# A graph layer on one NeuronCore: two folds of 1024 words become one of 2048, without a second place to fold into

## What is computed

```python
def layer(cur, incidence_m):
    mask = incidence_m > 0
    head = mask.astype(incidence_m.dtype)
    head = head / jnp.maximum(jnp.sqrt(jnp.sum(head * head, axis=-1, keepdims=True)), EPS)
    inc = incidence_m + head
    edge_fea = inc @ cur
    edge_degree = jnp.sum(inc, axis=-1, keepdims=True)
    return edge_fea / edge_degree

h = jnp.maximum(_layernorm(x, axis=-1), 0.0)
x = x + layer(h, adj)
```

## Time and profile before

| | |
|---|---|
| median of 3 runs | 1268.14 us (1267.59 to 1268.84) |
| profiled execution | 1278.49 us, its span 1276.7 us |
| DVE busy | 1189.2 us, 93% |
| ACT busy | 975.5 us, 76% |
| PE busy | 959.0 us, 75% |
| POOL busy | 791.1 us, 62% |
| DMA, moved | 471.00 MB, mean 369 GB/s |

### The profile page before, as it was taken

How to read it: one execution, slowest core, us unless ns; L and a number is a source line. 1 busy time by engine, 2 the same in 40 slices (tenths; PEclk the granted TensorE clock), 3 DMA queues, 4 the chain that set the end, 5 groups by cost and what they waited for, 6 DMA issues and landing times.

```text
span 1276.7 us, 14660 instructions
## 1 busy us (share of the span) xinstructions
PE 959.0 (75%) x2680; PEld 478.1 (37%) x2682; DVE 1189.2 (93%) x2868; ACT 975.5 (76%) x1902; POOL 791.1 (62%) x748
## 2 busy tenths in 40 slices
PE   0003878888888878787988887978878888977677
PEld 0001434444444444443434443434444434433343
DVE  6679999998999999998999999999999999999961
ACT  6657787887887988786888877888877888884731
POOL 1003667676666777776766767777776776765562
PEclk9999899898988989899898989999989988987888
DMA  9999999999999999999999999999999999997532
GB/s 356 427 422 406 396 394 388 369 387 369 379 378 382 401 373 401 395 401 394 402 400 401 392 374 384 399 400 395 402 396 402 402 397 373 401 390 275 175 106 74
DMA packets 148207, 471.00 MB, mean 369 GB/s; under 512 B 24826, under 2 KB 24826, under 8 KB 143965
## 3 DMA queue, kind: packets, MB, share of 16 engines
q1 hardware_dynamic: 90368, 331.38, 66.3%
q0 software_dynamic: 57744, 138.64, 29.7%
HBM read 490.47 MB, written 33.82 MB: 411 GB/s over the span
## 4 chain that ended last, share of the span: by engine, by line
DVE 55%; issue 17%; DMA 11%; ACT 6%; PE 6%; another core or an unknown queue 2%; SPq 1%; POOL 0%; DVEq 0%; ACTq 0%; POOLq 0%
DVE cand_word L794 17%; DVE folded L772 16%; DMA adj_tile<-in_adj_dram 8%; DVE cand_index L798 6%; DMA gathered_rows<-in_x_dram 3%; PE acc L1326 3%; DVE cand_index L817 2%; DVE cand_word L812 2%; ACT junk L573 2%; ACT adj_tile L560 2%; ACT diag L636 1%; PE acc L1337 1%; DVE diagonal_alone L779 1%; DVE entry L961 1%
## 5 line engine op out<-in xcount | busy, mean ns | idle before, releaser
L494 POOL DMA_INDIRECT gathered_rows<-h_scratch,slot_column x520 | 559.9, 1077 | 263.1 <-issue 158.0
L573 ACT ACTIVATE junk<-adj_tile,zero_unit 128x2048 bf16<-128x2048 f32 x256 | 510.0, 1998 | 48.3 <-issue 27.5
L1326 PE MATMUL acc<-gathered_rows,diag 128*128 128x512 f32 x1040 | 489.6, 622 | 21.4 <-DMA gathered_rows<-h_scratch,slot_column 18.2
L494 POOL DMA_INDIRECT gathered_rows<-h_scratch,spill_column x198 | 223.1, 1127 | 195.0 <-ACT spill_column L619 135.2
L794 DVE MAX8 cand_word<-folded 128x8 f32<-128x1024 f32 x244 | 298.2, 1222 | 5.9 <-remote 1.3
L772 DVE SCALAR_TENSOR_TENSOR folded<-adj_tile 128x1024 f32<-128x1024 f32 x244 | 296.1, 1214 | 7.7 <-DMA adj_tile<-in_adj_dram 5.6
L1326 PEld LDWEIGHTS acc<-gathered_rows,diag 128*128 128x128 f32 x1040 | 203.8, 204 | 263.4 <-issue 262.6
L798 DVE FIND_INDEX8 cand_index<-cand_word,folded 128x8 uint32<-128x1024 f32 x244 | 297.3, 1219 | 0.0
L1337 PE MATMUL acc<-gathered_rows,spill_matrix 128*128 128x512 f32 x396 | 186.8, 609 | 46.0 <-DMA gathered_rows<-h_scratch,spill_column 42.4
L636 ACT ACTIVATE diag<-ident,weights_and_payload 128x128 f32<-128x128 f32 x581 | 176.2, 388 | 16.0 <-issue 6.5
L1337 PEld LDWEIGHTS acc<-gathered_rows,spill_matrix 128*128 128x128 f32 x396 | 72.8, 192 | 154.8 <-issue 154.6
(11 more groups left out here) (151 smaller groups left out, 880.1 us busy)
## 6 DMA issues: line engine op xcount, KB each, us to landing
adj_tile<-in_adj_dram SPq DMA_DIRECT2D x256, 1024.0 KB
h_scratch<-adj_tile SPq DMA_DIRECT2D x16, 1024.0 KB, 10.6
out_dram<-out_tile SPq DMA_DIRECT2D x64, 256.0 KB
gathered_rows<-in_x_dram SPq DMA_DIRECT2D x12, 1024.0 KB, 12.6
x_residual<-in_x_dram SPq DMA_DIRECT2D x48, 256.0 KB
gathered_rows<-h_scratch,slot_column POOLq DMA_INDIRECT x520
x_held<-in_x_dram SPq DMA_DIRECT2D x4, 1024.0 KB, 7.9
gathered_rows<-h_scratch,spill_column POOLq DMA_INDIRECT x198, 3.5
```

The lines of the kernel that those rows point to most:

```text
L494: nc.gpsimd.indirect_dma_start(out=into, out_offset=None, in_=h[:, :], in_offset=bass.IndirectOffsetOnAxis(ap=column, axis=0), bounds_chec ...
L573: nc.scalar.activation(junk[:, n % 2].rearrange("p (j c) -> p j c", j=2), both[:, :, half], ACT.Relu, bias=zero_unit[:], scale=-UP, accum_ ...
L1326: last = nc.tensor.matmul(acc[t % 3][:], diag[:, t % 2, 1 + s], slot(t % 2, s), start=False, stop=False)
```

## The change

In each of the 61 folded tiles two folds take the place of four. `fold(t, k)` waits for chunks 2k and 2k + 1 and folds both in one operation of 2048 words, which fills both places of `folded`. So it also waits for the search of the chunk just before it, where a fold waited for the search of the chunk two before. The second fold of a period stands where the third stood; the fourth, between `heads` and `incs`, and the second, between `take_entry` and `columns_any`, are gone. The searches stay at 1024 words. In the diff's line numbers, those of the kernel after are two higher from the middle of `fold` on.

```diff
@@ load_chunk
-                        sp.wait_ge(folded, CHUNKS * (t - 2) + j + 1)
+                        sp.wait_ge(folded, 2 * (t - 2) + j // 2 + 1)
@@ fold
-            def fold(t, j):
-                dve.wait_ge(adj_loaded[t % 2][j], 16 * turn(t))
-                if CHUNKS * t + j >= 2:
-                    dve.wait_ge(idx_found, CHUNKS * t + j - 1)
-                a = chunk(t % 2, j)
-                nc.vector.scalar_tensor_tensor(out=F[:, j % 2], in0=a[:, 1], scalar=UP, in1=a[:, 0],
+            def fold(t, k):
+
+                for j in (2 * k, 2 * k + 1):
+                    dve.wait_ge(adj_loaded[t % 2][j], 16 * turn(t))
+                if 2 * t + k >= 1:
+                    dve.wait_ge(idx_found, CHUNKS * t + 2 * k)
+                a = A[:, t % 2, 4 * CW * k:4 * CW * (k + 1)].rearrange("p (j h c) -> p j h c", j=2, h=2)
+                nc.vector.scalar_tensor_tensor(out=F[:], in0=a[:, :, 1], scalar=UP, in1=a[:, :, 0],
                                                op0=ALU.mult, op1=ALU.add).then_inc(folded, 1)
-                if j == diag_chunk(t):
+                if k == diag_chunk(t) // 2:
                     read_diagonal(t)
                     cut_diagonal(t)
@@ cut_diagonal
-                dve.wait_ge(folded, CHUNKS * t + diag_chunk(t) + 1)
+                dve.wait_ge(folded, 2 * t + diag_chunk(t) // 2 + 1)
@@ find_values
-                dve.wait_ge(folded, CHUNKS * t + j + 1)
+                dve.wait_ge(folded, 2 * t + j // 2 + 1)
@@ period
                 if pick:
                     take_entry(r)
-                fold(t, 1)
                 if small:
                     columns_any(p)
                     ranks(p)
@@ period
                     pay_columns(p)
-                fold(t, 2)
+                fold(t, 1)
                 find_values(t, 2)
                 find_places(t, 2)
                 if small:
                     heads(p)
-                fold(t, 3)
                 if small:
                     incs(p)
                 find_values(t, 3)
```

## The result

The changed kernel takes 1272.64 us (median of 7 runs, 1270.72 to 1273.31), the kernel before 1268.58 in runs taken beside them (7 runs, 1267.28 to 1271.67). The ratio is 1.0028, with an interval of 1.0017 to 1.0039: 4.1 us slower. The profiled execution took 1273.31 us, its span is 1271.6.

What follows compares the result with a forecast made beforehand. DVE was taken to set the pace, busy 234 of 240 us. Fresh wait and folds 5.4, less 2.0 for diagonal tiles, plus 2.5 at the start gave 5.9: 1268.14 to 1274.0 us, 80% range 1267.5 to 1279.

Steps and rivals of the forecast that it cites:

- The large fold, heads and incs: Both pairs of a tile: 0.06 gained on the first, 0.07 lost on the second by incs waiting uncovered; 0.01 lost.
- The fresh wait: First fold of a pair waits for the search just before: 0.08 lost per tile; with both pairs 0.09, 5.4 us.
- The diagonal in chunk 3: In 13 tiles, fold to MAX8 and heads to MAX8 shorten by 0.16 more than in ordinary tiles: 2.0 us gained.
- The start: Tile 0: fold and search of chunk 2 fall behind chunk 3's arrival; 2.5 us lost, upper bound 4.6.
- Loads: Chunk loads in mid-run, needed up to 4 us earlier: nothing counted; timed runs taken as paced by DVE.
- case 2: Late in the run, chunk waits absorb up to 4.3 us of delay, the end at least 2.7 later: 1270.8; chance 0.15.
- Case 3: Before each fold, the small operation ahead hides the second wait: +1.1 us, 1269.2; chance 0.18.
- case 5: In each fold, the operation over two pieces costs more than its words, say 12 us: 1286; chance 0.07.
- Case 4: On DVE only the operation count matters, 122 fixed costs go without new waits: 4.8 us faster, 1263.3; chance 0.12.
- the rule weighed in the prediction: Trainium skill on DVE: a semaphore after each operation costs nothing extra, since the engine drains anyway; minimize op count.

Runs made afterwards that it cites:

- found_first: Changed kernel with the fold's three waits reordered, idx_found written ahead of the two chunk loads; 1282.59 us, ratio 1.0109 to the kernel before.
- three_places: Changed kernel with three places for folded chunks, so a fold waits for the search before the last, and one place of junk; 1281.68 us, ratio 1.0097.
- three_10: three_places with one gather per tile left out (10 instead of 11), for timing only; 1262.12 us, ratio 0.9946 to the kernel before.
- before_10: Kernel before with one gather per tile left out (10 instead of 11), for timing only; 1261.33 us, ratio 0.9941 to the kernel before.
- start_10: Changed kernel with 10 gathers per tile and tile 0 folded chunk by chunk, on a slower chip; 1276.47 us, ratio 0.9962 to the kernel before.
- before_again: Kernel before, unchanged, run again for a second profile; 1268.80 us, ratio 0.9999.
- heads_early: Changed kernel with heads moved from behind the search of chunk 2 to just behind the second fold; 1271.17 us, ratio 1.0018.

## Why the prediction was right, and where it was not

The direction and the range held. The number, 1274.0, is 1.4 us off, but two of its steps were wrong by more, in opposite directions: DVE's own loss is 9.9 us and not 5.9, and late loads took about 5 of it back where none was counted. That the number came so near is luck.

- **The large fold, heads and incs.** Right. 2.295 us for 2.28, 0.36 from `head` to MAX8 for 0.35; the fixed cost saved and the uncovered wait cancel, as the sum said.
- **The fresh wait.** Right in kind, mis-sized. "I take the step of 0.10 from rows 8" was the term; it is 0.14, twice per tile, so 0.16 and not 0.08, and the ordinary period is 0.155 longer where 0.09 was forecast. The bound written beside it (0.15, "if a third semaphore adds as much again as the second did") is what happened. Over 60 tiles that is 9.3 us instead of 5.4, just inside the bound of 9.6. `found_first` shows that it isn't only the number of semaphores: the late one stood last of three. That `three_places` and `found_first` both restore 16.97 to 17.00 shows that nothing else is in it.
- **The diagonal in chunk 3.** Right: these periods went from 17.02 to 17.04, where ordinary ones grew by 0.155, so 0.135 each and 1.8 us for 13 tiles, against 2.0. `three_10`, without the fresh wait, shows the saving by itself: 16.86 for these periods, and 17.02 in `before_10`.
- **The start.** The number is right, 2.5 forecast and 2.4 to 2.5 measured, but its path is only one of two that give it. The forecast put it all on the fold and search of chunk 2 behind chunk 3 of tile 0. `start_10` takes that away, and tile 1 still begins at 100.98, because its fold waits 3.79 us for the second chunk of its pair. The prediction named that arrival only as an upper bound (4.6). That both end at the same time is luck too.
- **Loads.** Here a step failed. "I take it (a choice) that most of that difference is such waits, so that the timed runs are paced by DVE, and the sum holds for them": the waits of rows 2 are absent from the second execution, those of rows 3 are larger in it. An execution at the median waits 7.2 us for late loads. So the mechanism of case 2 is what happened, larger than it was written (4.3 at most). Its own condition, less than 7.0 of delay at tile 59, was not met. DVE's own sum is 9.3 - 1.8 + 2.4 = 9.9, and with one gather less the time grows by 9.8. From tile 4 to tile 60 DVE takes 7.15 longer with one gather less, and 2.07 longer with all (961.57 in `before_again`, 963.64 in the kernel after), so 5.1 were absorbed; the waits themselves differ by 4.5. With the 3.68 that lay between the two at tile 4 (0.8 of it a chunk that came later in that execution) this is the delay of 5.75 at tile 60. Of these, 4.7 stand in the two spans (1266.9 and 1271.6) and 4.1 in the medians. The difference is at the very end: the last store of `out_tile` is issued 6.1 later (1254.60 and 1260.68), but the POOL operation that waits for it starts only 4.7 later (1259.46 and 1264.15).
- **Case 3** (the second wait hidden) fell with the step of 0.14, **case 5** (dearer words) with 2.295 us. **Case 4**, only the count of operations: `inc` starts 0.18 behind `head` and not 0.06, and moving `heads` alone gives 0.20 per period. So the rule weighed in the prediction does not hold for these waits.
- **What the prediction didn't see.** Beside DVE, late loads bound part of the run, and they explain 5.7 of the 12 us that `heads_early` should have given. The share of the DMA engines, 1.02 in the window that the prediction began with the earlier trace rows, doesn't tell this: it is 1.02 in `before_10` too, where no load is late. And POOL, at 170 of 240, was taken as free; it isn't any longer.

That one gather less removes all late loads speaks for the transfers' total rate as their cause. Which transfer delays which chunk wasn't tried.

## What to carry to other kernels

When operations are merged into one buffer, price the wait that becomes fresh, not the operation that goes: here 0.06 us was saved twice per tile and 0.08 lost twice, beside 0.13 for a wait that a removed fold had covered. If several semaphores guard an operation, the one that is met last may be cheaper at the front of the list. And before a gain on the busiest engine is counted as time, look for the second bound (here DVE's waits for loads late in the run, which a second profile showed better than the first) and for what a longer operation does to its neighbours.

## What the hardware showed beyond that

**A long two-input operation of DVE holds POOL's gathers.** Timeline of POOL in the kernel after; DVE's folds run from 503.99 to 506.30 and from 512.33 to 514.62, MAX8 and FIND_INDEX8 from 509.64 to 512.19:

```profile
503.98 1.00 POOL L494 DMA_INDIRECT gathered_rows<-h_scratch,spill_column  x1 [0.30 <-DVE slot_column L883]
505.28 1.89 POOL L494 DMA_INDIRECT gathered_rows<-h_scratch,spill_column  x1 [0.30 <-issue]
...
510.08 1.00 POOL L494 DMA_INDIRECT gathered_rows<-h_scratch,slot_column  x1 [0.30 <-issue]
511.38 0.99 POOL L494 DMA_INDIRECT gathered_rows<-h_scratch,slot_column  x1 [0.30 <-issue]
512.68 2.81 POOL L494 DMA_INDIRECT gathered_rows<-h_scratch,slot_column  x1 [0.30 <-issue]
```

A gather takes 1.00 us. One that starts inside a fold ends 0.87 behind the fold's end (507.17 and 506.30, 515.49 and 514.62), and all but one of the 119 gathers of this kernel that start inside a fold end 0.86 to 0.89 behind it. One that starts 0.01 ahead of the fold isn't held, and the searches hold none. In `before_again` the same 0.87 stands behind a short fold, which ran from 505.23 to 506.45:

```profile
505.93 1.39 POOL L494 DMA_INDIRECT gathered_rows<-h_scratch,slot_column  x1 [0.30 <-issue]
```

With folds of 1.2 us up to 1.0 is lost for one gather, with 2.3 us up to 2.1 (the longest gathers take 2.00 in `before_again` and 3.13 in the kernel after). In the Trainium skill, the page "SBUF — State Buffer" (section "Who interferes with whom") says that an instruction of DVE with two inputs in SBUF contends with an instruction of GpSimd that reads SBUF, and that the order of issue decides which of the two blocks the other. The trace agrees on the gathers: the fold has two inputs, the gather reads its row numbers there, and the searches have one input. It shows no block the other way: 93 of the 99 folds that start while a gather runs start 0.13 or 0.14 behind the search, as those do that meet none, and they last 2.29 to 2.32 where the others last 2.29. That the inputs are the cause, and not another property of the fold, no run here separates. The longer gathers of `found_first` in its bad stretch (194.23 over 148, 1.31, against 1.24 in the kernel after) follow from the same hold: the gather that a fold catches begins 0.41 into it, against 0.77 in the kernel after, so it is held for longer.

**Order of waits.** With the same three semaphores a fold starts 0.14 behind the end of the search when the late one is written last, and 0.05 to 0.08 behind it when it is written first.
